# Three of eight memory heads read as whole tables instead of two, with gathers that hold eight tokens of one head

## The chip, the cores and the metric

The kernel runs on one core of one Trainium2 chip. The metric is the time of one execution on the device, in microseconds (us). The engines of the core are named PE (TensorE, the matrix engine), DVE (VectorE), ACT (ScalarE), POOL (GpSimd) and SP (SyncE, which here only issues transfers).

## The reference

The input holds 16 sequences of 750 steps with 64 features. Two tanh layers, a scaled square, two more tanh layers and a strided filter make 375 tokens of each. What follows is residual: a retention layer, a memory layer of 8 heads, a layer that takes one AdamW step on the gradient of a small network over all tokens of all sequences and reads the network with queries, and a gated choice of one of 8 small networks. The change touches the memory layer alone:

```python
# per token and head: the best 16 of 64 x 64 keys, from the best 16 of each half
sim = einsum('pbnhd,pkhd->pbnhk', q, pk_keys)
scores, idx = top_k(sim, 16)
score = scores[0][..., :, None] + scores[1][..., None, :]       # 16 x 16
final_scores, pk_idx = top_k(score, 16)
final_scores = softmax(final_scores)
k = einsum('bnhk,bnhkd->bnhd', kv_scores, keys_table[ind])      # 4096 rows a head
v = einsum('bnhk,bnhkd->bnhd', kv_scores, values_table[ind])
attn = softmax(causal(einsum('bihd,bjhd->bhij', q, k)))         # over the tokens
out = einsum('bhij,bjhd->bhid', attn, v)
```

## The kernel before, in words

A sequence has 375 tokens in three tiles of 125. For each token and head the kernel needs a weighted sum of 16 rows (key and value side by side, 128 numbers) out of a table of 4096 rows. It finds that sum in two ways.

**Gathered heads.** For six heads, POOL issues indirect transfers that fetch the chosen rows from HBM (`L429`). One gather fetches 128 rows, one for each partition. Eight gathers make a *group*; a tile needs 94 gathers (12 groups), a sequence 282 (36 groups). A ring of nine groups (`RING`) holds fetched rows. PE multiplies each gather with a narrow matrix of weights `wbd` (8 columns, `L615`) and gives the place in the ring back by the semaphore `freed`, for which POOL waits. After every six groups ACT copies the sums out of the PSUM bank `gath` to `kvT` (`keep_half`, L988 to L992), and the next group's matmuls wait for that copy.

**Whole-table heads.** For two heads (`HD`), the table lies in on-chip memory and is multiplied whole with a dense matrix of weights, 128 rows of the table at a time: 32 chunks a head, 64 *steps* a sequence. In a step PE multiplies ranks with a fixed pattern (`L464`), ACT turns that by Relu into `past` (L902), PE adds three parts of the pair scores and `past` (`L469` three times, `L470`), ACT takes the exponential (`dense_w`, L910), and PE multiplies the result with the chunk of the table in fp32 (`L477`). So each step passes twice between PE and ACT; the steps overlap by one.

**The pick.** For each tile DVE picks the 16 best (`L1236` to `L1349`): four `max`, `find_index` and `match_replace` rounds, then for pairs of gathered heads an xor and a minimum over 125x1600 (L1313, L1317), for each half of a whole-table head an xor and a minimum over 125x1024 (L1323, L1327), the softmax's division, and at its end copies of the indices that PE has turned (`turn_picks`, L597 and L599; L1346 to L1349). POOL copies these to `idx_now` (L419) and issues the gathers.

**The order.** It is written out by hand, and each engine runs its list in order. A loop over 14 sequences carries nearly all of the time. One iteration b goes: `attention(b)`, with the pick of tile 2 of sequence b+1 on DVE under it; `turn_picks` for that tile; `turn(b+1)` (ranks and pair scores of b+1); `prepare(b+2)` (tokens, filter, retention); `similarities` of tile 0; `gradient(b)`; then `turn_picks` 0, `similarities` 1, `turn_picks` 1, `similarities` 2. The steps and groups of sequence b+1 have no time of their own: they are filled in between. The tables `FILL_TURN`, `FILL_PREPARE`, `FILL_GRADIENT`, `FILL_FIRST` and `FILL_SECOND` say how many (steps, groups) stand in each slot; `FILL_FIRST` stands between the gradient and `turn_picks` 0, while DVE picks tile 0, and `FILL_SECOND` between `similarities` 1 and `turn_picks` 1, while DVE picks tile 1. In a slot a group and a step alternate while there are both, and the rest of the steps follow. `STEPS_A`, `STEPS_B` and `GROUPS_INSIDE` put further ones into the heads of the attention.

These lines make a slot:

```python
for i in range(max(steps, groups)):
    if i < groups:
        take_group(b, at_group[0] // GROUPS, at_group[0] % GROUPS)
        at_group[0] = (at_group[0] + 1) % (NT * GROUPS)
    if i < steps:
        dense_steps(b, 1)
```

## Time and profile before

| | us |
|---|---|
| median of 3 runs (lowest, highest) | 9001.16 (8988.16, 9004.75) |
| the profiled execution's own time | 8921.69 |
| its span, from the first to the last instruction | 8919.9 |

| engine | busy us | share of the span |
|---|---|---|
| PE matmul | 5811.1 | 65% |
| PE weight load (overlaps) | 3849.5 | 43% |
| POOL | 4374.7 | 49% |
| DVE | 3250.8 | 36% |
| ACT | 2088.5 | 23% |

No engine is busy all the time. The mean granted clock of PE was 0.66 of full. A matmul's duration in the trace depends on the clock of its moment, so PE's busy time is work at a changing speed. POOL's busy time is that of issuing gathers (0.94 us each), not of the data on their way. An idle time before an instruction is put down to a releaser; "remote" (in the chain: "another core or an unknown queue") means that the profile names no instruction that ended just before, and "issue" that the engine waited for nothing that the profile shows.

### The profile page before, as it was taken

To read this page: it belongs to the slowest core of one execution; us is meant where nothing else is said; L and a number is where in the kernel's file an instruction comes from. 1 tells how busy PE (TensorE), PEld (TensorE's weight loads), DVE (VectorE), ACT (ScalarE), POOL (GpSimd) and SP (SyncE) were. 2 spreads that over 40 slices of the span, in tenths; PEclk is the share of its full clock that TensorE was granted. 3 is DMA by queue.
4 is the path that set the end of the run, shared out by engine and by line. 5 is a ranking of instruction groups with operands and counts; after the bars stand their busy time and mean duration, and the time that the engine had idled before them with its cause. 6 is when DMAs were issued, how large, how long until landed. Compare 5 with 4: busy or idle time off the path is not lost.

```text
span 8919.9 us, 86784 instructions
## 1 busy us (share of the span) xinstructions
PE 5811.1 (65%) x23616; PEld 3849.5 (43%) x23616; DVE 3250.8 (36%) x14095; ACT 2088.5 (23%) x4517; POOL 4374.7 (49%) x4574
## 2 busy tenths in 40 slices
PE   1367576575766757676665767667576666757677
PEld 1244444353444534444443544445344443534443
DVE  4334242433423243342424334232433423243036
ACT  0112122121322213132221312222131222222143
POOL 3454545545454554545455454545545445554500
PEclk9567566666756667675666667566666756666577
DMA  1111111111111111111111111111111111111100
GB/s 41 51 41 32 39 34 37 44 31 39 30 40 35 39 41 32 41 31 41 35 38 42 32 40 32 39 35 40 40 31 39 33 36 38 39 36 32 41 12 14
DMA packets 166480, 321.90 MB, mean 36 GB/s; under 512 B 82044, under 2 KB 90836, under 8 KB 165774
## 3 DMA queue, kind: packets, MB, share of 16 engines
q0 software_dynamic: 144384, 295.20, 12.5%
q1 hardware_dynamic: 21230, 20.00, 0.8%
q8 instruction: 232, 3.80, 0.2%
q14 instruction: 346, 2.83, 0.1%
q10 hardware_dynamic: 288, 0.07, 0.0%
HBM read 310.37 MB, written 4.61 MB: 35 GB/s over the span
## 4 chain that ended last, share of the span: by engine, by line
PE 36%; another core or an unknown queue 25%; issue 20%; DVE 14%; ACT 5%; DVEq 0%; ACTq 0%; DMA 0%; SPq 0%
PE gath L615 7%; PE accu L477 5%; PE dense L469 4%; PE work L668 2%; PE dense L464 2%; PE sims L662 2%; ACT past L902 2%; PE dense L470 1%; PE work L643 1%; PE work L698 1%; PE work L544 1%; PE work L655 1%; DVE front L1244 1%; DVE i L1243 1%
## 5 line engine op out<-in xcount | busy, mean ns | idle before, releaser
L429 POOL DMA_INDIRECT store<-in,idx_now x4512 | 4358.2, 966 | 3970.7 <-PE gath L615 2195.0
L615 PEld LDWEIGHTS gath<-wbd,store 128*128 128x128 f32 (+1 forms) x9024 | 1607.2, 266 | 783.7 <-issue 747.5
L615 PE MATMUL gath<-wbd,store 128*128 128x8 f32 (+1 forms) x9024 | 1553.7, 304 | 551.5 <-issue 432.8
L469 PE MATMUL dense<-parts_f,hot 128*128 128x375 bf16 x3072 | 905.0, 416 | 495.3 <-issue 420.7
L477 PE MATMUL accu<-dense_w,store 128*128 128x375 f32 x2048 | 1123.8, 640 | 11.9 <-issue 10.1
L902 ACT ACTIVATE past<-dense,edge 128x375 bf16<-128x375 f32 x1024 | 587.0, 573 | 2176.3 <-remote 1338.9
L464 PE MATMUL dense<-ranksT,hot 128*128 128x375 bf16 x1008 | 407.8, 405 | 847.1 <-ACT past L902 678.7
L469 PEld LDWEIGHTS dense<-parts_f,hot 128*128 128x128 bf16 x3072 | 322.2, 114 | 894.0 <-issue 820.6
L910 ACT ACTIVATE dense_w<-dense 128x375 f32<-128x375 f32 x1024 | 493.8, 482 | 887.3 <-remote 547.3
L464 PEld LDWEIGHTS dense<-ranksT,hot 128*128 128x128 bf16 x1008 | 158.4, 157 | 1083.0 <-issue 1033.7
L477 PEld LDWEIGHTS accu<-dense_w,store 128*128 128x128 f32 x2048 | 500.1, 258 | 142.2 <-issue 107.6
L470 PE MATMUL dense<-past,far 128*128 128x375 bf16 x1024 | 428.4, 418 | 7.8 <-issue 7.8
L1346 DVE CAST idx_next<-work 96x93 uint32<-96x93 f32 x48 | 12.1, 251 | 999.9 <-remote 675.2
L1194 DVE COPY h<-work 125x192 f32<-125x192 f32 x16 | 5.7, 358 | 977.1 <-PE work L544 643.6
L544 PE MATMUL work<-tapdiag,mixed 128*125 128x64 f32 x768 | 178.6, 384 | 192.3 <-issue 190.3
L668 PE MATMUL work<-shared 125*64 125x375 f32 (+2 forms) x768 | 265.8, 498 | 17.2 <-issue 12.4
L1317 DVE TENSOR_REDUCE idxf<-picks 125x32 f32<-125x1600 uint32 x144 | 262.1, 1820 | 25.9 <-DVE picks L1313 8.4
L544 PEld LDWEIGHTS work<-tapdiag,mixed 128*125 128x125 f32 x768 | 171.5, 310 | 198.3 <-issue 198.1
L1327 DVE TENSOR_REDUCE ranks<-picks 125x64 f32<-125x1024 uint32 x192 | 234.2, 1220 | 25.6 <-DVE picks L1323 5.8
L662 PE MATMUL sims<-kvT,two_q 64*125 64x125 f32 (+2 forms) x768 | 220.6, 426 | 23.6 <-ACT two_q L1015 11.6
L668 PEld LDWEIGHTS work<-shared 125*64 125x64 f32 x768 | 122.9, 177 | 188.9 <-issue 175.2
L1374 DVE TENSOR_TENSOR shared<-sims,mask 125x750 f32<-125x750 f32 x64 | 59.8, 935 | 390.5 <-PE sims L662 378.1
(285 smaller groups left out, 6983.9 us busy)
## 6 DMA issues: line engine op xcount, KB each, us to landing
store<-in,idx_now POOLq DMA_INDIRECT x4512
x_in<-in SPq DMA_DIRECT2D x16, 187.5 KB
store<-in SPq DMA_DIRECT2D x1, 2048.0 KB, 8.7
queries_kept<-n3T SPq DMA_DIRECT2D x16, 93.8 KB
h_saved<-h SPq DMA_DIRECT2D x16, 93.8 KB
store<-queries_kept SPq DMA_DIRECT2D x16, 93.8 KB, 2.4
store<-h_saved SPq DMA_DIRECT2D x16, 93.8 KB
out<-store SPq DMA_DIRECT2D x16, 93.8 KB
```

The source lines that it names most:

```text
L429: nc.gpsimd.indirect_dma_start(rows[0:slots, r * PER + i, :], None, kv_table, bass.IndirectOffsetOnAxis(ap=idx_now[0:slots, at:at + 1], ax ...
L464: mm(dense[:, 0, 0:S], hot[:, (i + 1) % CHUNKS, :], ranksT[:, (i + 1) // CHUNKS, :], start=True, stop=True).then_inc(s["dense_d"], 1)
L469: mm(dense[:, 1, 0:S], hot[:, c, :], parts[:, k, h, :], start=(k == 0), stop=False)
L470: mm(dense[:, 1, 0:S], far[:], past[:, i % 2, :], start=False, stop=True).then_inc(s["dense_m"], 1)
L477: last = mm(accu[:, 0, 0:S], table[:, h, c, :], dense_w[:, (i - 1) % 2, :], start=(c == 0), stop=(c == CHUNKS - 1))
L544: last = mm(work[0:P, 0, t * D:(t + 1) * D], mixed[:, at:at + STRIDE * (P - 1) + 1:STRIDE], tapdiag[:, k, :], start=(k == 0), stop=(k == T ...
L615: last = mm(gath[:, 0, at:at + 8], rows[0:slots, r * PER + i, :], wbd[0:slots, t * GATHERS + n, :], start=True, stop=True)
L662: last = mm(dst, qT[:, h % 2, tile(i)], kvT[0:D, h, 0:(i + 1) * P], start=True, stop=True)
L668: last = mm(work[D:128, 0, j * P:S], vo[:, j, h * D:(h + 1) * D], pT[:, min(j, 1), (0, 0, 2 * P)[j]:(S, 2 * P, S)[j]], start=(h == 0 and j ...
L902: fn(past[:, n % 2, :], dense[:, 0, 0:S], ACT.Relu, bias=edge[:, 0:1]).then_inc(s["dense_u"], 1)
L910: fn(dense_w[:, i % 2, :], dense[:, 1, 0:S], ACT.Exp).then_inc(s["dense_e"], 1)
L1317: v.tensor_reduce(idxf[:, at], pick, AX_X, ALU.min).then_inc(s["pick_step"], 1)
```

## The change

`HD` goes from 2 to 3: a third head is read as a whole table, so 96 steps a sequence instead of 64, and five heads are gathered. A gather now holds eight tokens of one head (8 x 16 rows) where it held one token slot of up to eight heads; a tile takes 80 gathers (10 groups), a sequence 240 (30 groups). The ring goes from nine groups to six. For the new order of rows DVE spreads the indices and weights over eight columns (`i_wide`, `w_wide`, with one more semaphore `w_done`), and `turn_picks` becomes ten small matmuls; POOL's copy and `idx_next` go, and DVE writes `idx_now` itself after a wait on `freed`. The copies out of PSUM become plain. The third head's ranks and pair scores use the bank `accu`. `upd` moves into `picks`. All fill tables change.

```diff
-HD = 2
+HD = 3
-GATHERS = 3 * QUADS + 1
+GATHERS = HG * BLOCK
-RING = 9
+RING = 6
-FILL_TURN = ((0, 0), (0, 0))
-FILL_PREPARE = ((2, 2), (1, 2), (2, 1), (1, 2), (2, 1), (1, 2), (2, 1), (1, 1), (2, 0))
-FILL_GRADIENT = ((3, 1), (0, 1), (0, 0), (0, 1), (2, 1))
-FILL_FIRST = ((5, 2), (3, 2))
-FILL_SECOND = ((11, 6), (7, 4))
-GROUPS_INSIDE = (0, 0, 1, 1, 1, 1, 1, 1)
+FILL_TURN = ((0, 2), (0, 1))
+FILL_PREPARE = ((1, 1), (1, 1), (1, 1), (1, 1), (2, 1), (1, 0), (2, 0), (1, 0), (1, 0))
+FILL_GRADIENT = ((2, 1), (1, 0), (1, 0), (1, 1), (1, 1))
+FILL_FIRST = ((13, 3), (8, 2))
+FILL_SECOND = ((20, 5), (13, 4))
+GROUPS_INSIDE = (0, 1, 1, 1, 1, 1, 0, 0)
-FIRST_HEAD, STEPS_A, STEPS_B = 2, (1, 1, 1, 1, 1, 1, 0, 0), (2, 2, 2, 2, 2, 2, 0, 0)
+FIRST_HEAD, STEPS_A, STEPS_B = 2, (1, 1, 1, 1, 1, 1, 0, 0), (3, 3, 3, 3, 3, 3, 0, 0)
...
             with nc.gpsimd.Fori(0, B) as b:
                 for t in range(NT):
                     pool.wait_ge(s["next_ready"], b * NT + t + 1)
-
-                    nc.gpsimd.tensor_copy(idx_now[:, gathers(t)], idx_next[:, gathers(t)]).then_inc(s["idx_taken"], 1)
-                    pool.wait_ge(s["idx_taken"], b * NT + t + 1)
                     for g in range(GROUPS):
...
-                for c, src in enumerate((wgt[:, 0:HG].rearrange("p h k -> p (h k)"), idxf[:].rearrange("p h k -> p (h k)"))):
-                    tr(work[0:HG * K, c, 0:P], src, ident[0:P, 0:P])
-                    for m in range(3):
-                        last = mm(work[HG * K:SLOTS, c, tile(m)], src[:, m * 32:(m + 1) * 32], ident[0:P, 0:P], start=True, stop=True)
+                for c, src in enumerate((w_wide, i_wide)):
+                    for h in range(HG):
+                        last = mm(work[:, c, h * BLOCK:(h + 1) * BLOCK], src[:, h].rearrange("p m k -> p (m k)"), eights[:, EIGHT:], start=True, stop=True)
...
-                nc.scalar.copy(ranksT[:], dense[:, :, 0:S]).then_inc(s["rank_done"], 1)
+                nc.scalar.copy(ranksT[:, 0:2], dense[:, :, 0:S])
+                nc.scalar.copy(ranksT[:, 2], accu[:, 0, 0:S]).then_inc(s["rank_done"], 1)
...
-                v.tensor_tensor(wgt[:], wgt[:], esum[:, 1, :].unsqueeze(2).broadcast_to([P, H, K]),
-                                ALU.mult).then_inc(s["wgt_done"], 1)
+                v.tensor_tensor(i_wide, idxf[:].unsqueeze(2).broadcast_to([P, HG, EIGHT, K]),
+                                eights[:, 0:EIGHT].unsqueeze(1).unsqueeze(3).broadcast_to([P, HG, EIGHT, K]), ALU.mult)
+                v.tensor_tensor(wgt[:, 0:HG], wgt[:, 0:HG], esum[:, 1, 0:HG].unsqueeze(2).broadcast_to([P, HG, K]),
+                                ALU.mult).then_inc(s["w_done"], 1)
+                dve.wait_ge(s["w_done"], n)
+                v.tensor_tensor(w_wide, wgt[:, 0:HG].unsqueeze(2).broadcast_to([P, HG, EIGHT, K]),
+                                eights[:, 0:EIGHT].unsqueeze(1).unsqueeze(3).broadcast_to([P, HG, EIGHT, K]), ALU.mult).then_inc(s["wgt_done"], 1)
                 yield
                 dve.wait_ge(s["tw_mm"], n)
                 if not (isinstance(b, int) and b == 0):
-                    dve.wait_ge(s["idx_taken"], b * NT + (t + 1 - NT))
...
+                    dve.wait_ge(s["freed"], b * (NT * GROUPS) + ((t + 1 - NT) * GROUPS + RING))
+                v.tensor_copy(idx_now[:, gathers(t)], work[:, 1, 0:GATHERS]).then_inc(s["next_ready"], 1)
```

Counted over an iteration, the steps and groups stand so (steps/groups): `turn` 0/0, now 0/3; `prepare` up to the filter (L544) 6/7, now 4/4; `prepare` after it 8/5, now 7/1; gradient 5/4, now 6/3; `FILL_FIRST` 8/4, now 21/5; `FILL_SECOND` 18/10, now 33/9; attention 20/6, now 26/5. The 65th (now 97th) step holds only the last L477.

The second half of `prepare` in the loop, PE's list from the rotation's matmuls to the retention's scores. Before (L615 is a group, L464 to L477 a step, `halves` and `two_q` the operands of the rotation and the scores, L86 a register's arithmetic):

```order
L556 MATMUL work<-halves,wrope_s 64x375
L557 MATMUL sims<-halves,wrope_s 64x375
L615 MATMUL gath<-wbd,store 128x8 x8
L86 REGISTER_ALU
L464 MATMUL dense<-ranksT,hot 128x375
L469 MATMUL dense<-parts_f,hot 128x375 x3
L470 MATMUL dense<-past,far 128x375
L477 MATMUL accu<-dense_w,store 128x375
L86 REGISTER_ALU
L464 MATMUL dense<-ranksT,hot 128x375
```

The same place of the changed kernel (its lines stand three later):

```order
L559 MATMUL work<-halves,wrope_s 64x375
L560 MATMUL sims<-halves,wrope_s 64x375
L89 REGISTER_ALU
L467 MATMUL dense<-ranksT,hot 128x375
L472 MATMUL dense<-parts_f,hot 128x375 x3
L473 MATMUL dense<-past,far 128x375
L480 MATMUL accu<-dense_w,store 128x375
L89 REGISTER_ALU
L467 MATMUL dense<-ranksT,hot 128x375
```

The group is gone from between the rotation and the steps; five groups stood after the filter before, and one stands there now.

PE's list around the end of `FILL_FIRST`: the last step, `turn_picks` 0 and the start of the second round. Before (`wgt` the weights, `idxf` the indices, `sims` the next tile's similarities):

```order
L470 MATMUL dense<-past,far 128x375
L477 MATMUL accu<-dense_w,store 128x375
L597 MATMUL work<-ident,wgt 96x125
L599 MATMUL work<-ident,wgt 32x125 x3
L597 MATMUL work<-ident,idxf 96x125
L599 MATMUL work<-ident,idxf 32x125 x3
L585 MATMUL sims<-simw,n2T 125x512 x2
L86 REGISTER_ALU
L615 MATMUL gath<-wbd,store 128x8 x8
```

The changed kernel at that place:

```order
L473 MATMUL dense<-past,far 128x375
L480 MATMUL accu<-dense_w,store 128x375
L601 MATMUL work<-eights,picks 128x16 x10
L588 MATMUL sims<-simw,n2T 125x512 x2
L616 MATMUL gath<-wbd,store 128x8 x8
```

Eight matmuls of up to 125 columns became ten of 16. What stands ahead of this place grew from 8 steps to 21, and DVE's wait for `turn_picks` 0 ends only behind them.

DVE's list at the end of the pick of tile 2, under the attention (`h` is the attention's own output). Before:

```order
L1327 TENSOR_REDUCE ranks<-picks 125x64
L1332 TENSOR_REDUCE esum<-wgt 125x8
L1334 COPY zsum<-esum 125x2
L1335 COPY ztop<-f 125x2
L1336 RECIPROCAL esum<-esum 125x8
L1338 TENSOR_TENSOR wgt<-wgt,esum 125x128
L1397 TENSOR_TENSOR h<-h_now,work 125x192
```

The changed kernel:

```order
L1395 TENSOR_TENSOR h<-h_now,work 125x192
L89 REGISTER_ALU
L1321 TENSOR_TENSOR picks<-places_s,keys 125x1024
L89 REGISTER_ALU
L1325 TENSOR_REDUCE ranks<-picks 125x64
L89 REGISTER_ALU
L1330 TENSOR_REDUCE esum<-wgt 125x8
L1332 COPY zsum<-esum 125x3
L1333 COPY ztop<-f 125x3
L1334 RECIPROCAL esum<-esum 125x8
L1336 TENSOR_TENSOR picks<-idxf,eights 125x640
```

The attention's output stood behind the whole pick and stands now ahead of its last pair; the rest of the pick, with the two wide products (the second one follows), comes after the attention's end.

## Rows read from the trace of the kernel before

**Rows 1.** The page, section 4: the chain that ended last, by engine

```profile
PE 36%; another core or an unknown queue 25%; issue 20%; DVE 14%; ACT 5%; DVEq 0%; ACTq 0%; DMA 0%; SPq 0%
```

**Rows 2.** The page, section 5, three groups (columns: busy, mean ns | idle before, releaser)

```profile
L429 POOL DMA_INDIRECT store<-in,idx_now x4512 | 4358.2, 966 | 3970.7 <-PE gath L615 2195.0
L902 ACT ACTIVATE past<-dense,edge 128x375 bf16<-128x375 f32 x1024 | 587.0, 573 | 2176.3 <-remote 1338.9
L464 PE MATMUL dense<-ranksT,hot 128*128 128x375 bf16 x1008 | 407.8, 405 | 847.1 <-ACT past L902 678.7
```

**Rows 3.** Windows: one iteration cut in seven (stretch, length, busy, clock, DMA, GB/s)

```profile
3571.30:3640.20 68.90, 49.84 (x178) 30.94 (x177) 8.71 (x34) 15.49 (x28) 40.97 (x45) 0.60 0.16 42
3640.20:3695.30 55.10, 32.32 (x126) 22.66 (x127) 40.13 (x242) 12.14 (x21) 18.27 (x19) 0.56 0.11 29
3695.30:3747.50 52.20, 31.38 (x153) 20.59 (x153) 14.48 (x17) 12.39 (x28) 34.22 (x37) 0.74 0.18 46
3748.40:3880.70 132.30, 68.94 (x291) 47.24 (x291) 50.31 (x241) 21.56 (x46) 81.85 (x87) 0.61 0.17 44
3881.00:3999.80 118.80, 105.39 (x441) 65.78 (x441) 71.01 (x305) 44.70 (x117) 50.57 (x47) 0.76 0.10 26
3999.80:4016.80 17.00, 14.15 (x52) 9.58 (x52) 3.88 (x8) 6.63 (x13) 0.00 (x0) 0.60 0.02 5
4016.80:4090.80 74.00, 47.61 (x195) 37.34 (x196) 0.65 (x2) 11.05 (x22) 47.90 (x51) 0.55 0.17 45
sum 518.30, PE 349.61 PEld 234.14 DVE 189.16 ACT 123.97 POOL 273.78; mean PE 49.94 PEld 33.45 DVE 27.02 ACT 17.71 POOL 39.11
```

**Rows 4.** Steps at the full clock: timeline of PE (start, us, names)

```profile
8472.22 0.32 PE L464 MATMUL dense<-ranksT,hot 128*128 128x375 bf16 x1
...
8475.12 0.32 PE L464 MATMUL dense<-ranksT,hot 128*128 128x375 bf16 x1
```

**Rows 5.** Steps at the half clock: timeline of PE

```profile
8354.24 0.52 PE L464 MATMUL dense<-ranksT,hot 128*128 128x375 bf16 x1
...
8357.05 0.43 PE L464 MATMUL dense<-ranksT,hot 128*128 128x375 bf16 x1
```

**Rows 6.** Two groups of gathers, at the full and the half clock: timeline of PE

```profile
8116.07 1.95 PE L615 MATMUL gath<-wbd,store 128*128 128x8 f32 x16
...
8209.66 3.42 PE L615 MATMUL gath<-wbd,store 128*128 128x8 f32 x16
```

**Rows 7.** End of the second picking round: timelines of POOL, PE, ACT and DVE

```profile
3834.20 0.94 POOL L429 DMA_INDIRECT store<-in,idx_now  x1 [9.08 <-PE gath L615]
...
3862.91 0.94 POOL L429 DMA_INDIRECT store<-in,idx_now  x1 [0.30 <-issue]
3868.80 0.94 POOL L429 DMA_INDIRECT store<-in,idx_now  x1 [4.94 <-remote]
...
3840.93 1.40 PE L615 MATMUL gath<-wbd,store 128*128 128x8 f32 x12
...
3868.10 0.39 ACT L988 COPY kvT<-gath 128x270 f32<-128x270 f32 x1 [18.43 <-remote]
...
3869.31 0.47 PE L464 MATMUL dense<-ranksT,hot 128*128 128x375 bf16 x1 [16.83 <-ACT past L902]
...
3880.48 0.25 DVE L1346 CAST idx_next<-work 96x93 uint32<-96x93 f32 x1 [41.66 <-remote]
```

**Rows 8.** Windows of the start: first prepare, picks of tiles 0 and 1; last attention

```profile
26.60:56.40 29.80, 20.10 (x76) 11.78 (x75) 9.83 (x33) 1.84 (x5) 0.00 (x0) 1.00 0.02 9
57.40:104.00 46.60, 0.00 (x0) 0.00 (x0) 45.47 (x233) 1.83 (x3) 0.00 (x0) 1.00 0.00 0
113.50:238.50 125.00, 0.00 (x0) 0.00 (x0) 49.06 (x233) 0.48 (x2) 66.71 (x71) 1.00 0.14 38
...
8509.48:8570.07 60.59, 58.98 (x257) 32.02 (x258) 21.20 (x57) 37.17 (x99) 0.00 (x0) 0.96 0.00 1
```

**Rows 9.** The page, section 5: two groups of the pick on DVE

```profile
L1317 DVE TENSOR_REDUCE idxf<-picks 125x32 f32<-125x1600 uint32 x144 | 262.1, 1820 | 25.9 <-DVE picks L1313 8.4
L1327 DVE TENSOR_REDUCE ranks<-picks 125x64 f32<-125x1024 uint32 x192 | 234.2, 1220 | 25.6 <-DVE picks L1323 5.8
```

More of the change, by code:

```diff
@@ L612, in take_group @@
                     n = g * PER + i
-                    slots = SLOTS if n < GATHERS - 1 else HG * K
-                    at = (n - half * HALF_AT) * 8
-                    last = mm(gath[:, 0, at:at + 8], rows[0:slots, r * PER + i, :], wbd[0:slots, t * GATHERS + n, :],
+                    at = (n - half * HALF_AT) * EIGHT
+                    last = mm(gath[:, 0, at:at + EIGHT], rows[:, r * PER + i, :], wbd[:, t * GATHERS + n, :],
                               start=True, stop=True)
@@ L989, in keep_half @@
[L989 to L993 removed]
+                whole = slice(0, HG // 2) if half == 0 else slice(HG // 2 + 1, HG)
@@ new lines, in keep_half @@
+                at = 0 if half == 0 else SLOTS // 2
+                src = gath[:, 0, at:at + HG // 2 * SLOTS].rearrange("p (h n) -> p h n", n=SLOTS)
+                nc.scalar.copy(kvT[:, whole, tile(t)], src[:, :, 0:P])
+                if half == 0:
+                    nc.scalar.copy(kvT[:, HG // 2, t * P:t * P + SLOTS // 2],
+                                   gath[:, 0, HG // 2 * SLOTS:HG // 2 * SLOTS + SLOTS // 2]).then_inc(s["kv_done"], 1)
+                else:
+                    nc.scalar.copy(kvT[:, HG // 2, t * P + SLOTS // 2:(t + 1) * P],
+                                   gath[:, 0, 0:P - SLOTS // 2]).then_inc(s["kv_done"], 1)
```

98 lines of the change are left out of this document (43 added, 55 removed).

## The prediction, made before the changed kernel ran

> **What bounds the kernel now.** I read the chain of waits first [rows 1]. PE holds 36% of it, 25% ends on a releaser that the profile doesn't name, 20% is issue, DVE has 14%. So no engine is the bound by itself; a good part is waiting between engines. The groups of the page show who waits [rows 2]: POOL stands 2195 us before gathers for PE's groups (the ring is full), PE's first matmul of a step waits 679 us for ACT's Relu, and that Relu waits 1339 us for "remote".
>
> Then I cut one iteration into stretches [rows 3]: 518.3 us, the sum row. Only in the attention (118.8 us) is PE nearly full, 105.4 us at clock 0.76. In the second picking round (132.3 us) PE works 68.9 us, DVE 50.3 us, and 87 gathers are issued: nobody is full.
>
> What "remote" is, one place shows [rows 7]. PE's last group starts at 3840.93 and runs 1.40 us. ACT's copy of these sums, which needs nothing else, starts at 3868.10, 26 us later, and its Relu and PE's next step (3869.31, 16.83 us idle) are late with it. In between POOL issues gathers without a break from 3834.20 to 3862.91, 24 of them 1.248 us apart (28.71 us by 23), then stops, and all is delivered. DVE, whose pick was ready, waits 41.66 us and reads at 3880.48: PE's list ends the round, not DVE. The start says the same [rows 8]: picking tile 0 without gathers takes 46.6 us, picking tile 1 under gathers 125.0 us, with equal work (233 instructions, 45.5 and 49.1 us busy). So a gather stream slows every handshake beside it, and a step has two with ACT.
>
> A page of the Trainium skill speaks against this reading: SBUF — State Buffer, section "SBUF: two separate sides", says that engines and DMA can't contend there except at the port that VectorE and GpSimd share, or at the DMA's own ports. By it ACT's late copy could not come from gathers, and taking them out of `prepare` would give only their matmuls, 8 to 14 us instead of the 30 below. The 26 us of ACT, which doesn't use that port, speak for a delay in delivery, on which the page says nothing.
>
> **Prices.** A step costs PE 1.45 us at the full clock (two between 8472.22 and 8475.12) [rows 4] and 2.81 at the half clock [rows 5]; at a mean clock c I take 1.45/c. A group costs 1.95 to 3.42 us of PE [rows 6] and 8 x 1.248 = 10.0 us of POOL.
>
> **The change, stretch by stretch, for one iteration.** The counts are those of the change's section.
>
> *Attention:* 6 steps more, one group less. PE is the bound here (89% busy), so this counts in full: 6 x 1.45/0.76 = 11.4, less 2.4, is +9. Ends: 8.7 - 2.0 = +7 (full clock) and 16.9 - 3.4 = +13 (half).
>
> *turn:* the pick of tile 2 no longer fits under the attention. Behind the attention's output DVE now has an xor and a reduction (1.22 each [rows 9], 2.4), and two products of 640 elements. No row shows these; between nothing and a row of 1024 elements, 1.22, I take 0.9 each. With the hop `w_done` this is about +5, and all waits for it, for `turn_picks` 2 stands behind. The third head adds 3 transposes and 4 matmuls on PE, 3 copies on ACT, 1 subtraction on DVE: `turn` takes 17.0 us for two heads [rows 3], half of that for one would be 8.5, nothing the other end; most is fixed hops, so +4. Together +9 (+4 to +14).
>
> *First half of prepare* (4016.8 to 4090.8): with `turn`, seven groups stand ahead of the filter as before. Two steps fewer at clock 0.55: -5 (0 to -10).
>
> *Second half of prepare* (3571.3 to 3640.2): one step and four groups fewer. PE's work falls from 49.8 by 2.4 and 4 x 2.8 to 36. The four last slots have no group and POOL, whose ring is now full, mostly stands; so handshakes should be short again. The whole of the first `prepare`, both halves, without gathers or steps takes 29.8 us [rows 8]. With 7 steps in half of it, 39 of the 68.9 us remain: -30. Ends: -14 (only the matmuls) and -38 (7 steps at 1.45 to 2.3 and half of 29.8).
>
> *Gradient:* a step more, a group less: 0. DVE is the busiest to its size here (40.1 of 55.1), and the pick of tile 0 runs in it and in the first round. The pick loses half a pair of 1.82 each (L1313, L1317) and gains two pairs of 1.22 [rows 9] and the wide products: -1.8 + 4.9 + 1.8 = +5, of which I let 2 through. In the second round DVE has 41.66 us to spare [rows 7], so there it is nothing.
>
> *First round* (3695.3 to 3747.5): 13 steps, one group. PE had 20.8 us idle of 52.2, but by the waits of steps and groups, which come again with each new one. 13 x 1.45/0.74 = 25.5, and 2.6: +28. Ends: +10 (half of the full-clock work goes into idle time) and +40 (13 x 2.81 and 3.42).
>
> *Second round* (3748.4 to 3880.7): 15 steps, less a group, at clock 0.61: 15 x 2.38 - 3 = +33 of work. PE was idle 63.4 us, much of it because steps stood still beside 87 gathers; one group less to issue gives 10 us of quiet. I let about half go into idle time: +15. Ends: -5 and +39 (15 x 2.81 - 3.4).
>
> Sum: 9 + 9 - 5 - 30 + 2 + 28 + 15 = +28 us. Fourteen iterations: +392. In the start the pick of tile 1 ran under 72 gathers; a ring of 48 ends 30 us sooner, 24 x 1.248; the second sequence's fills there take back some: -20. POOL's copy goes (it hid behind the full ring), the wait on `freed` for `idx_now` is met long before (the tile's groups of the last sequence are all taken by then), the table's third part loads under the first `prepare` and pick: nothing. 8921.7 + 372 = 9,294 on the profiled execution's account. The median of the runs shown is 0.9% above that execution, so I scale by 9001.16/8921.69: 9,376, and forecast **9,360**.
>
> **The rivals.**
>
> *Faster.* The change takes 42 of 282 gathers away, 52 us of POOL's issuing an iteration. If the delay goes with the gathers, and the added steps stand in long rows on PE, the clock rises. Rows for it: the last attention, without gathers and nearly full (59.0 of 60.6 us), ran at 0.96, and the first round has 0.74 where `prepare`, as idle, has 0.55 [rows 3, 8]. Then the first round costs +15, the second 0, `prepare` -36 in all, attention +7, turn +5, gradient -6: -15. 14 x -15 - 20 = -230, scaled 8,770. It decides where the 28 added steps of both rounds cost less than some 15 us together, 0.5 us each. Against it: the second round already had its PE list as the last to end. The page TensorE: Matmul & The Clock Gate, section "What's actually happening", says that the clock follows how busy the engine has lately been, which is this rival; the 0.96 agrees, the gradient's 0.56 at 59% busy beside the first round's 0.74 at 60% shows that a mean share doesn't settle it. Chance 0.24.
>
> *No change.* Savings in `prepare` at 38 and both rounds at about +22 together cancel: within 0.2%, 18 us. Chance 0.06.
>
> *Much slower.* The rounds run at the half clock, as steps that wait for ACT one by one might: +40, +35; attention +13, turn and gradient +11, `prepare` -25: +74, so 14 x 74 - 20 = +1,016, scaled 10,030; a mixture of this and my case gives 9,650 and above. Also here: a ring of six lets the data come late for PE, which the trace before, with nine, shows nowhere as a large wait. Chance 0.12.
>
> **How the numbers follow.** My own case (+1.5 to +6%, 9,140 to 9,550) has 0.48; a smaller loss 0.10; with the last rival slower is 0.70. Faster is 0.24, the same (within 0.2%, about what a measurement of this kernel tells from none) 0.06. To leave out 2 in 10 the range goes from 8,850, inside the faster case, to 9,620.
>
> **What would show it.** In the trace after, the iteration should be near 546 us: second half of `prepare` near 40 with POOL nearly idle, first round near 80, second near 147, attention near 128, `turn` near 26. Waits of PE's L467 for ACT grow in sum, POOL's wait for PE too. I am wrong if the rounds hold their 52 and 132 us within 15, or if PE's clock in them is 0.85 or more; or if `prepare` stays near 69, which would show that delays there are not the gathers'.

## The result, and the profile after

The changed kernel takes 9736.62 us, the kernel before, beside it, 8994.66 us: a ratio of 1.081, 95% interval 1.076 to 1.086. One of the changed kernel's four executions took 26,664 us; it stands in the median but not in the ratio. The forecast was slower, at 9,360, with a range of 8,850 to 9,620; the direction was right and the size was not.

The page of the changed kernel, section 4, the chain by engine:

```profile
PE 42%; another core or an unknown queue 28%; issue 14%; DVE 9%; ACT 7%; ACTq 0%; DVEq 0%; DMA 0%; SPq 0%
```

PE's share rose from 36% and the unnamed releasers' from 25% [rows 1]. The groups that answer to [rows 2], from section 5 of the same page (all lines stand three later, ACT's one):

```profile
L432 POOL DMA_INDIRECT store<-in,idx_now x3840 | 3693.7, 962 | 5524.5 <-PE gath L616 4018.0
L903 ACT ACTIVATE past<-dense,edge 128x375 bf16<-128x375 f32 x1536 | 881.2, 574 | 2582.6 <-remote 1527.6
L467 PE MATMUL dense<-ranksT,hot 128*128 128x375 bf16 x1520 | 572.2, 376 | 915.1 <-ACT past L903 747.5
```

POOL issues 672 gathers fewer and is busy 665 us less, but now stands 4018 us before PE's groups, where it stood 2195. Nobody uses the POOL time that was won. One iteration of the changed kernel in windows (stretch, length, busy time and count of PE, PEld, DVE, ACT and POOL, clock, DMA share, GB/s), cut at the same places as [rows 3]: second half of `prepare`, gradient, first round, second round, attention, `turn`, first half of the next `prepare`:

```profile
3841.10:3872.80 31.70, 22.17 (x84) 11.05 (x84) 8.65 (x34) 13.71 (x24) 7.54 (x8) 0.77 0.06 17
3872.80:3926.50 53.70, 32.32 (x131) 19.10 (x132) 40.45 (x240) 16.72 (x30) 12.49 (x13) 0.65 0.09 23
3926.50:4020.40 93.90, 53.53 (x250) 32.83 (x249) 19.27 (x22) 22.98 (x47) 48.79 (x52) 0.74 0.14 37
4023.80:4168.70 144.90, 88.98 (x397) 56.66 (x397) 54.94 (x244) 36.89 (x73) 68.53 (x72) 0.69 0.13 34
4169.00:4317.30 148.30, 120.80 (x471) 71.09 (x469) 71.46 (x301) 51.34 (x130) 40.57 (x40) 0.75 0.07 19
4317.30:4352.80 35.50, 27.60 (x107) 22.57 (x107) 8.96 (x16) 6.07 (x12) 12.91 (x14) 0.50 0.09 25
4352.80:4416.70 63.90, 36.79 (x168) 27.50 (x168) 0.84 (x2) 9.59 (x17) 40.68 (x43) 0.58 0.17 45
```

One stretch got even shorter than forecast, the second half of `prepare`: 31.7 us where it was 68.9, and 39 in the forecast. Against it stand the first round (93.9 for 52.2), the attention (148.3 for 118.8) and `turn` (35.5 for 17.0).

Single iterations differ by some us, so the rest of this text uses means over twelve iterations of a trace, cut at the same instructions of each (DVE's copy of the filter's output, ACT's copy of the first similarities, DVE's sum of gradients, its index copies of tiles 0 and 1, the attention's output, the last part of the pair scores). In us:

| | prepare 2 | gradient | first | second | attention | turn | prepare 1 | sum |
|---|---|---|---|---|---|---|---|---|
| before | 69.3 | 55.1 | 52.3 | 134.4 | 118.8 | 17.8 | 76.4 | 524.1 |
| after | 31.2 | 54.2 | 98.5 | 148.5 | 147.2 | 34.1 | 65.3 | 579.0 |
| difference | -38.1 | -0.9 | +46.2 | +14.1 | +28.4 | +16.3 | -11.1 | +54.9 |
| forecast | -30 | +2 | +28 | +15 | +9 | +9 | -5 | +28 |

Fourteen times 54.9 is 769 us, about the 799 by which the two profiled spans differ (9718.9 and 8919.9).

What a late hand-over looks like in the attention is seen in PE's timeline of the changed kernel, one head of the attention (start, us, engine, line; in brackets the idle time before):

```profile
4209.85 1.95 PE L616 MATMUL gath<-wbd,store 128*128 128x8 f32 x16
...
4216.76 0.64 PE L472 MATMUL dense<-parts_f,hot 128*128 128x375 bf16 x3
4217.24 0.32 PE L473 MATMUL dense<-past,far 128*128 128x375 bf16 x1
...
4219.90 0.32 PE L467 MATMUL dense<-ranksT,hot 128*128 128x375 bf16 x1 [1.71 <-ACT past L903]
4224.12 1.10 PE L472 MATMUL dense<-parts_f,hot 128*128 128x375 bf16 x3 [3.90 <-issue]
```

ACT's timeline of the same head (the Relu that L467 waits for, and the exponential that must end before L472):

```profile
4219.18 0.57 ACT L903 ACTIVATE past<-dense,edge 128x375 bf16<-128x375 f32 x1 [2.56 <-remote]
4223.49 0.48 ACT L911 ACTIVATE dense_w<-dense 128x375 f32<-128x375 f32 x1 [3.73 <-remote]
```

POOL's timeline of the same head (issuing of that head's group; the first row, and the first of the next group):

```profile
4212.61 0.94 POOL L432 DMA_INDIRECT store<-in,idx_now  x1 [54.93 <-PE gath L616]
...
4232.89 1.16 POOL L432 DMA_INDIRECT store<-in,idx_now  x1 [10.53 <-PE gath L616]
```

The group's matmuls free a place at 4211.8, and POOL issues eight gathers from 4212.61 on, for 10 us. The steps stand in the same 10 us. Two steps pass. The third waits 1.71 us for ACT's Relu and then 3.90 us, which the profile puts down to nothing, until ACT's exponential has ended at 4223.97. ACT was late itself: that exponential needs PE's L473, which ended at 4217.56, and starts at 4223.49. The granted clock fell to 0.50 within that pause, at 4220.6 us, and three L472 take 1.10 us, where they took 0.64.

`turn` on DVE (timeline), from the attention's output to the indices:

```profile
4317.51 0.35 DVE L1395 TENSOR_TENSOR h<-h_now,work 125x192 f32<-125x192 f32 x1 [4.16 <-PE work L706]
4318.02 1.23 DVE L1321 TENSOR_TENSOR picks<-places_s,keys 125x1024 uint32<-125x1024 uint32 x1
...
4321.79 0.83 DVE L1336 TENSOR_TENSOR picks<-idxf,eights 125x640 f32<-125x640 f32 x1
...
4329.45 0.24 DVE L1347 CAST idx_now<-work 128x80 uint32<-128x80 f32 x1 [5.72 <-PE work L601]
```

The last pair of the pick and both wide products (0.83 and 0.82; I had 0.9) stand behind the output. PE waits 7.44 us for them and then turns them in 4.42 us at the half clock. That pause is not why the clock is low: the trace grants 0.50 from 4302.5 to 4370.8 us, since before the attention's output.

### The profile page after: what moved, and what is told of

Same layout as the page of the kernel before. It is cut to its first block, busy times and chain, and to the rows that moved or that the text cites. A ratio compares the mean times of both kernels' runs of the same rounds, so it can differ in the third digit from the quotient of the medians.

```text
span 9718.9 us, 95311 instructions
## 1 busy us (share of the span) xinstructions
PE 6496.3 (67%) x26320; PEld 4080.6 (42%) x26320; DVE 3496.2 (36%) x14303; ACT 2615.2 (27%) x5445; POOL 3696.4 (38%) x3854
## 4 chain that ended last, share of the span: by engine, by line
PE 42%; another core or an unknown queue 28%; issue 14%; DVE 9%; ACT 7%; ACTq 0%; DVEq 0%; DMA 0%; SPq 0%
PE accu L480 8%; PE dense L472 8%; PE gath L616 6%; PE dense L473 3%; PE dense L467 3%; ACT past L903 2%; PE sims L663 2%; PE work L669 2%; PE work L601 2%; PE work L644 2%; PE sims L588 2%; PE work L699 1%; PE work L656 1%; ACT dense_w L911 1%
## 5 line engine op out<-in xcount | busy, mean ns | idle before, releaser
L432 POOL DMA_INDIRECT store<-in,idx_now x3840 | 3693.7, 962 | 5524.5 <-PE gath L616 4018.0
L472 PE MATMUL dense<-parts_f,hot 128*128 128x375 bf16 x4608 | 1256.8, 391 | 857.1 <-issue 663.3
L616 PEld LDWEIGHTS gath<-wbd,store 128*128 128x128 f32 x7680 | 1328.2, 259 | 615.8 <-issue 582.6
L480 PE MATMUL accu<-dense_w,store 128*128 128x375 f32 x3072 | 1564.4, 598 | 19.8 <-issue 15.4
L903 ACT ACTIVATE past<-dense,edge 128x375 bf16<-128x375 f32 x1536 | 881.2, 574 | 2582.6 <-remote 1527.6
L616 PE MATMUL gath<-wbd,store 128*128 128x8 f32 x7680 | 1285.1, 299 | 420.6 <-issue 363.0
L467 PE MATMUL dense<-ranksT,hot 128*128 128x375 bf16 x1520 | 572.2, 376 | 915.1 <-ACT past L903 747.5
L911 ACT ACTIVATE dense_w<-dense 128x375 f32<-128x375 f32 x1536 | 741.0, 482 | 1271.3 <-remote 753.5
L472 PEld LDWEIGHTS dense<-parts_f,hot 128*128 128x128 bf16 x4608 | 444.1, 109 | 1474.2 <-issue 1332.9
L480 PEld LDWEIGHTS accu<-dense_w,store 128*128 128x128 f32 x3072 | 697.0, 241 | 187.3 <-issue 127.8
L467 PEld LDWEIGHTS dense<-ranksT,hot 128*128 128x128 bf16 x1520 | 202.6, 133 | 1299.4 <-issue 1162.4
L473 PE MATMUL dense<-past,far 128*128 128x375 bf16 x1536 | 606.4, 395 | 8.2 <-issue 8.2
L473 PEld LDWEIGHTS dense<-past,far 128*128 128x128 bf16 x1536 | 178.6, 116 | 163.9 <-issue 102.6
```

The source lines that it names most:

```text
L432: nc.gpsimd.indirect_dma_start(rows[:, r * PER + i, :], None, kv_table, bass.IndirectOffsetOnAxis(ap=idx_now[:, at:at + 1], axis=0),).then ...
L467: mm(dense[:, 0, 0:S], hot[:, (i + 1) % CHUNKS, :], ranksT[:, (i + 1) // CHUNKS, :], start=True, stop=True).then_inc(s["dense_d"], 1)
L472: mm(dense[:, 1, 0:S], hot[:, c, :], parts[:, k, h, :], start=(k == 0), stop=False)
L473: mm(dense[:, 1, 0:S], far[:], past[:, i % 2, :], start=False, stop=True).then_inc(s["dense_m"], 1)
L480: last = mm(accu[:, 0, 0:S], table[:, h, c, :], dense_w[:, (i - 1) % 2, :], start=(c == 0), stop=(c == CHUNKS - 1))
L616: last = mm(gath[:, 0, at:at + EIGHT], rows[:, r * PER + i, :], wbd[:, t * GATHERS + n, :], start=True, stop=True)
```

## The experiments

Two theories were set against each other. **A**: gathers beside the steps delay the hand-overs between PE and ACT, the pauses bring the half clock, and so a step is dear where gathers are issued. **B**: a step costs PE's work, wherever it stands. **C**, for single runs: the rounds are held by the supply of gathers behind a ring of six.

**No gathers, changed kernel, twice.** Sequence 0 is still gathered. For the other sequences POOL runs a loop that only counts each group as there, and PE waits for the new count:

```diff
+            with nc.gpsimd.Fori(1, B) as b:
+                for t in range(NT):
...
+                        pool.wait_ge(s["freed"], b * (NT * GROUPS) + (t * GROUPS + g + 1))
+                        r = ring_of[t * GROUPS + g]
+                        nc.gpsimd.sem_inc(s["quiet"], 1)
```

> The changed kernel in which only sequence 0's rows are gathered; for the other 15 sequences POOL issues no transfers and only signals each group at once, so PE multiplies old rows (the output's gathered heads are those of sequence 0). Theory A (the added steps are dear because gathers beside them delay the hand-overs between PE and ACT, and the pauses bring the half clock): without the stream the first round falls from 98 us to under 60, the second from 148 to under 100, the attention from 147 to about 125, and the iteration from 579 to about 430. Theory B (the price is PE's work at whatever clock, the stream beside it is harmless): the rounds keep most of their length and the iteration stays above 530. Second half of prepare, which has few gathers already, stays within 3 us of its 31 by both.

**No gathers, kernel before.**

> The same for the kernel before: gathers for sequence 0 alone. Theory A: iteration from 524 us to 380 to 400; second half of prepare from 69 to 35 or less. The difference of the two kernels without gathers is then the plain price of 32 steps less 6 groups and of the longer turn: 32 x 1.45 - 6 x 1.95 + 12 = about +47 us an iteration, near the +55 measured with gathers, so that the stream costs both about the same in sum. Theory B: above 480, and the same +47 or more.

Measured: 6,831 and 6,231 us. But on this chip the kernel before, with all its gathers, took 6,373 us (7 runs, 6,372 to 6,382), not 8,995. Gathers cost it next to nothing there (142 us), and these two runs said nothing about the delay. They do give the price of the change without gathers, both on one chip: 600 us.

**Twelve steps moved, and the attention's six.** On the same chip:

```diff
-FILL_PREPARE = ((1, 1), (1, 1), (1, 1), (1, 1), (2, 1), (1, 0), (2, 0), (1, 0), (1, 0))
+FILL_PREPARE = ((1, 1), (1, 1), (1, 1), (1, 1), (2, 1), (4, 0), (5, 0), (4, 0), (4, 0))
-FILL_FIRST = ((13, 3), (8, 2))
+FILL_FIRST = ((6, 3), (3, 2))
```

> The changed kernel with 12 of the 21 steps of the first round moved into the last four slots of prepare, where no group stands. Theory A: a step costs 3.5 us in the first round (46 us by 13 steps and a group) and 1.5 to 2 us in the quiet half of prepare, so the first round loses some 40 us, prepare gains 18 to 24: 16 to 24 us less an iteration, 9,380 to 9,510 in all. Theory B: the same work at another place, within 0.5% of 9,737. Theory C (the first round is held by the supply of gathers, 5 groups of 10 us behind a ring of six, not by its steps): the first round hardly shortens, prepare grows, and the whole gets slower.

```diff
-FILL_PREPARE = ((1, 1), (1, 1), (1, 1), (1, 1), (2, 1), (1, 0), (2, 0), (1, 0), (1, 0))
+FILL_PREPARE = ((1, 1), (1, 1), (1, 1), (1, 1), (2, 1), (2, 0), (4, 0), (3, 0), (2, 0))
...
-FIRST_HEAD, STEPS_A, STEPS_B = 2, (1, 1, 1, 1, 1, 1, 0, 0), (3, 3, 3, 3, 3, 3, 0, 0)
+FIRST_HEAD, STEPS_A, STEPS_B = 2, (1, 1, 1, 1, 1, 1, 0, 0), (2, 2, 2, 2, 2, 2, 0, 0)
```

> The changed kernel with STEPS_B back at 2 a head; the six steps go into the last four slots of prepare. The heads take 107.6 us, 29.6 more than before. Theory A: the third step of a head falls into the 10 us in which POOL issues that head's group, waits for ACT up to 4 us and leaves PE at the half clock; the heads fall back by 20 to 30 us, prepare gains 9 to 12: 10 to 20 us less an iteration, 9,450 to 9,600. Theory B: six steps at 1.9 us are 11 us of the 29.6; moved they cost the same again, within 0.5% of 9,737.

Measured: 7,053 us (ratio 1.104, 1.101 to 1.108) and 6,953 us (1.091, 1.087 to 1.095). Both ratios are above the 1.081 of the change itself where gathers are dear, so with hardly any delay a kernel with a third whole-table head still doesn't pay; the changed kernel as it is was not run on this chip. All further runs were on chips where the kernel before took 8,926 to 8,956.

**Both kernels as they are**, the kernel before for its trace and the changed one for its ratio.

> The kernel before, unchanged, to have its trace beside the next runs: it took 6373 us in the last job where it took 8995 beside the changed kernel's result, and 6231 without gathers. If the difference is theory A's delay, missing on that chip, the trace shows each stage near that of the run without gathers (first round 26 us, second 58, prepare's second half 45), and no copy of ACT that starts tens of us after the matmul it needs. Where the job shows 9,000 again, the long rounds of the trace before should come back.

> The changed kernel, unchanged. If the kernel before takes about 6,370 here: without gathers the changed kernel took 6,831, so theory A, whose delay is absent, expects 6,900 to 7,050, a ratio of 1.08 to 1.11; theory B expects the ratio to be the plain price of the work, too, 1.09. If the kernel before takes 9,000, then 9,737 and 1.08 again. A ratio of 1.02 or less would say that the change is worth something else where gathers do not delay.

Measured: 8,908 us for the kernel before, 9,562 us for the changed one, ratio 1.070 (1.066 to 1.075). The stretches came back: first round 52.3 and 94.0 us, second 134.6 and 149.0, attention 118.4 and 143.1. The changed kernel's ratio thus varies by a per cent between chips.

**The layout alone**: `HD = 2`, ring of nine, the old tables, 96 gathers a tile:

```diff
-HD = 3
+HD = 2
-RING = 6
+RING = 9
...
```

> The other half of the change alone: gathers of eight tokens of one head, DVE's wide products, ten small matmuls, no copy by POOL, but two whole-table heads, 96 gathers a tile (94 before), the ring of nine and the fill tables of before. If the third head's steps are the whole loss, this one is within 1% of the kernel before (0.99 to 1.01: 6 gathers more in 282, and 2 to 3 us on DVE and PE for each tile). If the new layout costs something of its own (the pick's longer end in turn, 6 us an iteration), 1.01 to 1.02.

Measured: 9,082 us, 1.019 (1.014 to 1.023). So the layout costs a quarter of the loss, at its expected upper end, mostly in the first round (59.7 us for 52.3). The third head, its tables and the ring of six are the rest together; the changed kernel with a ring of nine was not run, so what the smaller ring costs is not shown.

**`turn` without groups:**

```diff
-FILL_TURN = ((0, 2), (0, 1))
+FILL_TURN = ((0, 0), (0, 0))
-FILL_PREPARE = ((1, 1), (1, 1), (1, 1), (1, 1), (2, 1), (1, 0), (2, 0), (1, 0), (1, 0))
+FILL_PREPARE = ((1, 2), (1, 2), (1, 1), (1, 1), (2, 2), (1, 0), (2, 0), (1, 0), (1, 0))
```

> The changed kernel with FILL_TURN empty, its three groups back in the first slots of prepare. In the trace after, the stretch from turn_picks 2 to the pair scores took 23.2 us where it took 13.1. If the groups are the larger part of these 10 us, it falls to 16 or less, while prepare up to the filter grows by about the same: within 0.5% of the changed kernel. If they keep PE's clock low there, 1% faster. If it stays at 20 or more, the third head's transposes, pair scores and copies are what makes turn long.

Measured: 9,725 us, 1.090 (1.086 to 1.094), where the changed kernel on that chip has 1.070. `turn` fell by 5.6 us, but `prepare` grew by 6.1 before the filter and 12.3 behind it. So the groups are a third of what `turn` gained (the other 10 us are the pick's end and the third head), and they stand better there than in `prepare`.

**No gathers once more, on a chip where they cost**, then the moves once more, and both together:

> The changed kernel with gathers for sequence 0 alone, once more, for the first time it ran where even the kernel before took 6,373 us with all its gathers, so it could not show what they cost where that kernel takes 8,900 to 9,000. Theory A: it takes 6,830 us again whatever the kernel before takes here; if that is 8,940, the delay comes with the gathers and is all of the 2,700 us between. If it takes over 8,000 here, the slowness of this chip has another source than the gathers and theory A falls.

> The changed kernel with 12 steps moved from the first round into the quiet half of prepare, once more. If the kernel before takes 8,940: theory A expects the first round 35 to 45 us shorter and prepare's second half 15 to 24 longer, a ratio of 1.04 to 1.05 where the changed kernel has 1.07. Theory B: 1.07. Theory C: first round within 10 us of 94, ratio over 1.08.

> The changed kernel with two steps a head again and six more in prepare, once more. If the kernel before takes 8,940: theory A expects the heads at 80 us (104 to 108 in the changed kernel), prepare's second half at 41 to 43 (it was 41.2), ratio 1.045 to 1.055. Theory B: the heads lose 12 us, prepare gains 10, ratio 1.07.

> Both moves: STEPS_B at 2, 12 steps out of the first round, all 18 in prepare's last four slots. If the kernel before takes 8,940: with theory A the two gains add, ratio 1.02 to 1.03, still slower than the kernel before, since 18 steps at about 1.9 us in prepare are 34 us of the 38 that it had won. Theory B: 1.07.

Measured: 7,063 us without gathers, so some 2,500 us of the 9,562 come with them. The moves: 9,449 us (1.058, 1.054 to 1.061), 9,475 us (1.061, 1.057 to 1.064), both 9,346 us (1.046, 1.041 to 1.050). Against the changed kernel's trace of the other chip, twelve steps out of the first round took 17.5 us off it and 10 off the second, and cost 19.3 in `prepare`: 2.3 us a step there and 1.6 here. Six steps out of the attention took 18.4 us off it, 3.1 a step, and cost 11.1, 1.85 a step. B, which had 1.07 for all three, falls; C falls too, since the first round did shorten. Both moves gave less than A had forecast.

The same two kernels had run on the chip where gathers cost next to nothing, and set beside each other the four traces say how much of a step's price is delay (means over twelve iterations, us):

| | prepare 2 | first | second | attention |
|---|---|---|---|---|
| twelve moved, gathers cheap | 48.9 | 28.4 | 89.8 | 130.5 |
| six moved, gathers cheap | 41.2 | 55.2 | 80.8 | 113.2 |
| twelve moved, gathers dear | 50.3 | 76.5 | 138.9 | 142.3 |
| six moved, gathers dear | 42.1 | 95.3 | 146.4 | 124.7 |

The twelve steps are in the rounds of the second and fourth row and not in those of the first and third. They cost both rounds together 17.8 us where gathers are cheap (55.2 + 80.8 less 28.4 + 89.8, 1.5 a step) and 26.3 where they are dear (2.2): about a third of their price is the delay. The attention's six cost 17.3 (130.5 less 113.2) and 17.6 us, 2.9 a step on both chips. So A is wrong for the attention: a third step in a head is dear with hardly any delay, and the delay there is 11.5 us with two steps a head (124.7 for 113.2) and 11.8 with three (142.3 for 130.5). And the prices differ by the stretch without any help of gathers, which B denied.

**The pair without gathers, half the number, half the height.** The last two from sequence 1 on, in a loop of its own; with half the number PE's counts are made to match:

> The kernel before with gathers for sequence 0 alone, once more, for its pair (the changed kernel so, 7,063 us) ran on a chip where gathers cost much. Expected 6,230 to 6,460 by theory A. The difference of the pair, 600 to 830 us, is then the plain price of the change without any gathers, and the gathers' own cost is about 2,600 us in the kernel before and 2,500 in the changed one: 42 gathers fewer of 282 give back only some 100 to 200 us, less than their share of 15% (390).

```diff
+                        for i in range(SIZES[g] // 2):
```

> The changed kernel with half the number: from sequence 1 on, of each group of eight only four gathers are issued (the other rows stay those of sequence 0). Between all gathers (9,562) and none (7,063). If the delay grows with the time that POOL issues without a break (bursts twice as short), more than half of the cost goes: 7,300 to 7,900. If it is in proportion: 8,300. If only whole bursts matter little and it is the number of groups: above 9,000.

```diff
+                                rows[0:64, r * PER + i, :], None, kv_table,
+                                bass.IndirectOffsetOnAxis(ap=idx_now[0:64, at:at + 1], axis=0),
```

> The changed kernel with gathers of half the height: from sequence 1 on each gather fetches 64 rows instead of 128 (the others stay those of sequence 0), the number of issues is the same. If a gather's issue takes less POOL time with fewer rows and the delay is that of issuing, it is near the run with half the number, 7,300 to 8,300; if the issue takes 1.25 us all the same and the delay comes from issuing, it stays above 9,200; if it takes 1.25 us all the same and the time falls to 8,300 or less, the data on their way are the cause, not POOL's issuing.

Measured: 6,356, 7,526 and 9,667 us. The means of an iteration now give each stretch its plain price and its delay:

| | prepare 2 | gradient | first | second | attention | turn | prepare 1 | sum |
|---|---|---|---|---|---|---|---|---|
| before, no gathers | 45.6 | 54.8 | 26.3 | 58.5 | 114.9 | 16.0 | 40.3 | 356.4 |
| after, no gathers | 30.5 | 54.2 | 52.9 | 77.3 | 128.3 | 34.1 | 25.7 | 403.0 |
| before (the run above) | 66.4 | 55.2 | 52.3 | 134.6 | 118.4 | 18.5 | 76.7 | 522.1 |
| after (the run above) | 31.0 | 54.2 | 94.0 | 149.0 | 143.1 | 34.0 | 64.5 | 569.8 |

The plain price of the change is 46.6 us an iteration (39 by the pair on the chip of 6,373 us, 358 and 397), and the gathers cost 165.7 us in the kernel before and 166.8 in the changed one: 42 gathers fewer of 282 gave nothing back. (By whole runs they cost 2,552 and 2,499 us. The four rows come from three chips, on which the kernel before took 8,938 to 8,956 us.) The delay left `prepare`'s second half (20.8 to 0.5) and went to the first round (26.0 to 41.1) and the attention (3.5 to 14.8). Half the number took 81% of their cost away (2,036 of the 2,499 us), half the height nothing, though it halved the bytes. It did not halve the packets, as the queue's line of the page (section 3: packets, MB, share of 16 engines) shows for the changed kernel and for half the height:

```profile
q0 software_dynamic: 122880, 251.90, 9.7%
q0 software_dynamic: 122880, 133.94, 5.7%
```

The issues from sequence 1 on, from section 5 of the page with half the number:

```profile
L447 POOL DMA_INDIRECT store<-in,idx_now x1800 | 1774.0, 986 | 4661.2 <-PE gath L634 4016.0
```

and of the page with half the height:

```profile
L447 POOL DMA_INDIRECT store<-in,idx_now x3600 | 3318.0, 922 | 5261.1 <-PE gath L631 3450.5
```

The issue of 64 rows takes 0.92 us, that of 128 took 0.96. So the delay goes with the number of gathers and not with their bytes. What of a gather it is, POOL's issuing, its 32 packets or the signals that it sends on landing, these runs don't tell apart, since half the height leaves all three as they were. The Trainium skill's page SBUF — State Buffer, section "SBUF: two separate sides", says that DMA and engines can't contend there; the run with half the height agrees (9,667 us for 9,562).

The traces also record when a semaphore was updated. In the place of [rows 7] no engine's update is recorded between 3849.77 and 3868.00 us; then five come within 0.1 us. Among them are those of an L464 that had ended at 3847.56 and of an L470 that had ended at 3851.23. POOL's last issue before it ended at 3863.85, and updates by landing gathers go on until 3865.19, so the end of the delay doesn't tell these two apart either. The traces lack some updates (of 576 by L615 they hold 510), so what follows is rough. Stretches of over 8 us without an engine's update, after the first 400 us, number 126 in the kernel before (1,539 us in sum) and 89 in the changed one (1,042 us), but 2 on the chip where gathers are cheap, in the run with twelve steps moved (18 us).

**Five groups of the kernel before in `turn`:**

```diff
-FILL_TURN = ((0, 0), (0, 0))
+FILL_TURN = ((0, 3), (0, 2))
-FILL_PREPARE = ((2, 2), (1, 2), (2, 1), (1, 2), (2, 1), (1, 2), (2, 1), (1, 1), (2, 0))
+FILL_PREPARE = ((2, 2), (1, 2), (2, 1), (1, 1), (2, 1), (1, 0), (2, 0), (1, 0), (2, 0))
```

> A try at a kernel faster than both: the kernel before with five of its groups taken in turn (0/3 and 0/2), where POOL otherwise waits with a full ring, and none in the last four slots of prepare; 7 groups instead of 12 in prepare. From the changed kernel, whose turn with three groups took 5.6 us more and spared 18 us in prepare: turn +9 to 12, prepare's second half -15 to -25, ratio 0.975 to 0.99. If groups cost the same wherever they stand, 1.00.

Measured: 9,027 us, 1.009 (1.006 to 1.013). The expectation was wrong: no time was won. Windows of one iteration, `turn` and the first half of `prepare`:

```profile
4030.70:4057.20 26.50, 23.82 (x103) 19.43 (x102) 3.65 (x8) 5.55 (x12) 12.18 (x14) 0.56 0.12 33
4057.20:4164.20 107.00, 47.31 (x230) 38.27 (x229) 0.91 (x2) 11.89 (x22) 69.53 (x75) 0.60 0.17 46
```

The second half of `prepare` did fall by 32 us (to 34.5), but its first half rose by 31 to 107.7: 11 groups now stand ahead of the filter, for 7, and 89 gathers are issued in these windows; that they delay this stretch instead is the reading that fits, not one that a run isolates.

**Rests for POOL.** The number of gathers stays; before each four POOL clears their places twice and waits for its own write:

```diff
+                            if i % 4 == 0:
+                                for k in range(2):
+                                    nc.gpsimd.memset(rows[:, r * PER + i:r * PER + i + min(4, SIZES[g] - i), :], 0.0).then_inc(s["prep"], 1)
+                                    pool.wait_ge(s["prep"], b * RESTS + (rests[t * GROUPS + g] + i // 4 * 2 + k + 2))
```

> The changed kernel with a rest for POOL before each four gathers: twice it clears the four places that they will fill (128x512 each, some 0.5 us) and waits for its own write. All gathers are issued, none is left out. Halving the number of gathers took 82% of their cost away. If what counts is the length of unbroken issuing, the rests let the waiting hand-overs through: bursts of 5 us, ratio to the kernel before at or under 1.00 where the changed kernel has 1.07 to 1.08. If what counts is the number of gathers, or the rests are too short to let anything through, the time stays within 1% of the changed kernel or grows, as each group takes 2 to 3 us more of POOL.

> The same rests in the kernel before, as a candidate for a kernel faster than both. If the length of unbroken issuing counts: ratio 0.85 to 0.95. If the number counts: 1.00 to 1.04, for POOL's stream grows from 10 to 12 or 13 us a group, 36 groups of 522 us an iteration.

Measured: the changed kernel 7,531 us, 0.844 (0.840 to 0.848) of the kernel before; the kernel before with rests 8,292 us, 0.929 (0.925 to 0.934). Both beat both kernels, and with rests in both the change is worth 7,531/8,292 = 0.908. POOL's timeline of the changed kernel with rests:

```profile
4106.17 0.54 POOL L434 MEMSET store<- 128x512 f32 x1
4106.86 0.53 POOL L434 MEMSET store<- 128x512 f32 x1 [0.15 <-issue]
4108.19 0.95 POOL L438 DMA_INDIRECT store<-in,idx_now  x1 [0.81 <-POOL store L434]
...
4112.88 0.54 POOL L434 MEMSET store<- 128x512 f32 x1
```

Four gathers now take 6.7 us with a rest of 2.0 us among them. Groups of its page (section 5), which answer to L903 and L467 above, and PE's gathers:

```profile
L909 ACT ACTIVATE past<-dense,edge 128x375 bf16<-128x375 f32 x1536 | 882.1, 574 | 1603.2 <-PE dense L473 1141.5
L473 PE MATMUL dense<-ranksT,hot 128*128 128x375 bf16 x1520 | 542.0, 357 | 59.9 <-ACT past L909 37.4
L622 PE MATMUL gath<-wbd,store 128*128 128x8 f32 x7680 | 1264.1, 302 | 467.4 <-DMA store<-in,idx_now 449.5
```

and the last of the same for the kernel before with rests:

```profile
L621 PE MATMUL gath<-wbd,store 128*128 128x8 f32 (+1 forms) x9024 | 1693.4, 325 | 1560.8 <-DMA store<-in,idx_now 1534.4
```

ACT's Relu now waits mostly for PE (1,142 us) and not for "remote" (1,528 us without rests), PE's first matmul waits 37 us for it instead of 748, and what is new is that PE waits for the rows themselves: 450 us in the changed kernel, 1,534 in the kernel before. A group now takes 2 x 6.7 = 13.4 us of POOL at least, the kernel before's 36 about 480 of its 483.4 us an iteration, the changed one's 30 are 402 of its 434.3. In this regime the gathers are the bound of the kernel before, and there 42 fewer are worth what I had hoped for. In the traces with rests one stretch of over 8 us without an engine's update is left in the changed kernel, none in the kernel before. The rests do two things at once: they end the unbroken issuing and they lower the rate, from one gather in 1.25 us to one in 1.68. Which of them helps was not separated.

## Why the prediction was wrong, step by step

The direction and the sign of each large term were right: the rounds, the attention and `turn` pay, `prepare` gains. The step that failed is how the sum treats the delay. It counts it as won in `prepare` (-30, where "only the matmuls" would be -14) and sizes what is added to the first round and the attention by PE's work alone; with -14 there the sum would have been +44, beside a plain price of 46.6 in the runs without gathers. The delay was won in `prepare`, 20.3 us of it, but it came back in other stretches, 15.1 us in the first round and 11.3 in the attention, and over the iteration it was 165.7 and is 166.8 us. The two terms where it came back, +28 and +9, measured +46.2 and +28.4; together that is 37.6 us more, and the whole miss is 26.9 (54.9 for 28).

- *"First round: +28"* measured +46.2. The plain price is 26.6 (the runs without gathers: 26.3 to 52.9), so 25.5 + 2.6 was well sized as work. The sum has no term for the delay, which grew by 15 us (26.0 to 41.1). That the added steps themselves bring it is shown in part only: with twelve steps fewer it is 97 us in both rounds together, with all of them 106.
- *"Attention: +9, PE is the bound, so this counts in full"* measured +28.4 (+24.7 in the later pair). Without gathers it is already +13.4, and the moves price a step there at 2.9 us, not at 1.45/0.76 = 1.9. That this is because the step stands between two transposes of a head's chain is a reading, not shown. The delay adds 11 us more, and it stays when the third step is taken out; why it stands there stays open.
- *"turn: +9"* measured +16.3. The end of the pick cost 6.6 us for my 5 (PE's turning starts 7.1 us after the attention's output, where it started 0.5 us after); the third head's +4 was right by what is left (16.3 - 6.6 - 5.6 = 4.1); three groups were not counted here at all but with the first half of `prepare`, and they take 5.6.
- *"First half of prepare: -5"*, measured -11.1, the counterpart of those groups.
- *"Second half of prepare: -30"*, measured -38.1: POOL almost still, as foreseen, and the delay gone whole (0.5 us left).
- *"Second round: +15"* measured +14.1, which is luck in part: without gathers it is +18.8, and the delay fell by 4.4. *"Gradient: +2"* measured -0.9.
- *The start: "-20"*. Outside the fourteen iterations the changed kernel is 30 us longer (799 - 769). The pick of tile 1 did end sooner, at 228.2 us where it ended at 243.4, by half of what was forecast; what else grew at the start and the end was not followed up.
- *The rival "Faster"* counted on 42 gathers fewer. They gave something only with rests (0.908 by the same change), and for another reason than it names: there POOL's stream bounds the kernel before.
- *The rival "Much slower"* put the rounds at the half clock; they ran at 0.74 and 0.69, as before at 0.74 and 0.61. The result lies at its lower edge without its cause. Its doubt about a ring of six, that data come late for PE, finds no support: PE's waits for gathered rows don't show among the main releasers of the changed kernel's L616. What the smaller ring does to the times at which POOL may issue was not tested.

Left open: why one chip hardly shows the delay, what of a gather holds back the other engines' signals, and why the delay moved from `prepare` to just these stretches.

## What to carry to other kernels

When hand-overs between engines start late beside POOL's issuing, space the issuing out before moving work about: short rests among the gathers were worth 7% and 21% (0.929, and 0.844 for 1.070), while moving steps was worth 2.3% (1.046 for 1.070). A delay that one stretch loses can come back in another, so count it over the whole loop. Price an added step by the stretch it will stand in and by the chain it will stretch, not by PE's work alone: 1.45 us of work cost 1.6 to 3.1 us here, and 2.9 us in the attention even where gathers cost next to nothing. A run without the suspected traffic, in both kernels, gives the plain price of a change and its delay apart, and should be the first one made.

## What the runs showed of the hardware

- Beside indirect gathers issued back to back (1.25 us apart) on POOL, the hand-overs between other engines come late: about 2,500 us of 9,562 in the changed kernel, 2,550 of 8,908 in the kernel before (6,356 without). Half the number of gathers took 81% of it in the changed kernel, half the rows of each (same packets, half the bytes) nothing. Rests of 2.0 us before every four took most of it there (7,531 us; 7,063 without gathers), and 634 us of it in the kernel before (8,292 for 8,926).
- It depends on the chip: on one of the five of the experiments the kernel before ran in 6,373 us, with POOL's gathers of the runs beside it as close together as elsewhere (1.25 us). The traces of that chip hold 16 landing updates a gather, those of the others with all gathers and no rests 4; what that means is open.
- In a pause of 3.9 us on PE the granted clock fell from 1.00 to 0.50, and the matmuls behind it took 1.10 us for three instead of 0.64.
